# First layer's loop: where the gate product and the projection stand, and how far ahead the decay scans run

## The chip, the core and the metric

The kernel runs on one core of one Trainium2 chip. The metric is the device time of one execution in microseconds (us). TensorE (PE, with PEld for its weight loads), VectorE (DVE), ScalarE (ACT), GpSimd (POOL) and the DMA queue of SyncE (SP) work through their own instructions in order and wait for each other by semaphores.

## What is computed

Two transformer layers on x of 4 batches x 256 tokens x 256 features, each with modulated layer norms. The first layer's attention is a gated delta rule with 32 value heads over 16 key heads; this is where the loop stands:

```
qkvz = h @ W_qkvz                      # q, k, v, z per key head
q, k, v = silu(causal conv of 4 taps over q, k, v)
step:  S = S * alpha_t                 # per token and head; S is 128 x 128
       v_new = (v_t - S'k_t) * beta_t
       S = S + k_t v_new' ;  o_t = S'q_t
og = o * silu(z);  og = og * rsqrt(mean(og*og) + eps) * norm_weight
out = og @ W_out
```

The rest (a feed-forward part with integer weights, a second layer with softmax attention and a sum of eight factors) isn't touched.

## The kernel before

Tokens are cut into two chunks of 128 (c = 0, 1). The recurrence of a chunk is a triangular system, whose inverse is built once per key head for all batches and heads. The loop `for kh in range(16)` has four steps b = 0..3, one per batch (B = 4), and each engine has its own step function: `pe_step`, `act_step`, `dve_step`, `pool_step`. A pass over the four steps is called a round here. The order inside a step is written out by hand; engines meet only at semaphores. Step b = 0 is the one that `merges`: it alone puts the inverse together from 32x32 blocks (`pe_merge_*`, lines 390 to 411), which POOL has computed during the round before (`pool_inverse`, lines 1045 and 1048, tiles Tn and tmp) and which came back by DMA.

In one step a batch is solved (`pe_solve` 0, 1, 2 at line 442; after 0 and 2 ACT copies Y by `act_y`, line 686, after 1 DVE makes R2, line 919), its output is formed (`pe_o` 0 and 1, lines 455 and 457; `dve_og`, line 927, multiplies with the silu of the gate z; `act_ss`, line 714, squares and sums it; `pool_ro`, line 1021, takes the root), and the batch of the step before, `last`, is normalised (`act_ogn`, 722), turned (`pe_ot`, 466; copied by `act_ots`, 745) and projected (`pe_f` 0 and 1, 476), then added up (`dve_acc`, 934). Beside it run preparations of later steps: the product for q and k eight to nine steps ahead (`pe_qk`, 314; `act_tap0` and `dve_tap` form the convolution, then `act_silu_qk`, 660 and 662), the gram matrices (`pe_gram0` at 324, `pe_gram1` at 328 and 332; scaled into BP by `dve_bp`, 915), v three steps ahead (`pe_v`, 344; turned by `pe_vt`, 366; copied by `act_vs`, 678) and the gate product z (`pe_z`, 354; `act_silu_z`, 667, into the tile named hT). The v and z products share a PSUM bank: `pe_z` waits for the taps of v, and the next `pe_v` for the silu of z.

`dve_bp` needs the decays E1 and E2 of its batch, running products of alpha that `dve_scan` makes by `tensor_tensor_scan` (lines 866 and 869): two of 128x256 and two of 128x128 for a batch, called a set here. There is one pair of buffers, so that the scans of a batch wait for the BP of the batch before it.

At the end of step 0 ACT and DVE also split the weights of later heads in a high and a low part (lines 732, 727 on ACT; 878, 874 on DVE). In steps 2 and 3 ACT copies half of the inverse turned (`act_turn`, 739). The loop of the ACT step that follows a merging step begins with `act_ss(*last)`, in front of `act_y` 0:

```
if last and merges(last[2]):
    act_ss(*last)
```

## Time and profile before

| | us |
|---|---|
| median of 3 runs (1215.8 to 1224.04) | 1216.73 |
| the profiled execution, its own time | 1216.18 |
| its span, first to last instruction | 1214.5 |
| one round of the loop, 577.20 to 633.37 | 56.17 |

The span begins at the first instruction; 1.7 us of the execution lie around it. Rounds are told apart by the first gram matmul of step 0. A row of a time line gives the start in us from the span's start, the time, engine, line, operation, output <- inputs and how many were put together; in square brackets how long the engine sat idle before it and for whom. A matmul's own time is longer than the distance to the next one's start, since they overlap: what a group takes of PE is the distance between starts.

### The profile page before, as it was taken

The page shows a single profiled execution, that of the slowest core. Times are in us where ns is not written, and L with a number is a line of the kernel's source. Part 1 is how long each engine was busy: PE and PEld are TensorE (multiplying, and loading weights), DVE is VectorE, ACT ScalarE, POOL GpSimd, SP SyncE. Part 2 cuts the span into 40 slices and gives each one's busy share as a digit, 9 for nine tenths or more (in the row PEclk, how much of TensorE's full clock was granted, in tenths as well). Part 3 has the DMA queues.
Part 4 walks back from the last instruction along what each step waited for, and adds up shares of the span by engine and source line. Part 5 has one row for each costly group of instructions (what it writes and reads, how often), then busy time and mean ns, then how long its engine had stood idle before and what let it go on. Part 6 is the DMA issues. An engine that isn't in the chain of part 4 may idle for free. (4 is left out here: it accounts for less than half of the span.)

```text
span 1214.5 us, 30101 instructions
## 1 busy us (share of the span) xinstructions
PE 1125.3 (93%) x10744; PEld 980.4 (81%) x10744; DVE 903.9 (74%) x2304; ACT 824.7 (68%) x2225; POOL 724.4 (60%) x1187
## 2 busy tenths in 40 slices
PE   7795799999999999999999999999998798998975
PEld 6685688888888888988888888888887787776654
DVE  6878587988888897989897898888792525328764
ACT  6333577777777777777777777877775665219983
POOL 3274677787878776877778787777676702114211
PEclk9778899999999999999999999999998989999998
DMA  5211315522231313141322313131215130002000
GB/s 185 64 57 29 94 39 82 56 69 58 65 92 41 82 41 82 41 106 45 82 55 67 62 62 92 40 82 32 48 34 158 27 112 1 1 6 70 2 19 18
DMA packets 140868, 72.80 MB, mean 60 GB/s; under 512 B 114184, under 2 KB 130064, under 8 KB 138800
## 3 DMA queue, kind: packets, MB, share of 16 engines
q1 hardware_dynamic: 140720, 70.88, 23.4%
q8 instruction: 86, 1.41, 0.5%
q14 instruction: 62, 0.51, 0.2%
HBM read 57.06 MB, written 13.78 MB: 58 GB/s over the span
## 5 line engine op out<-in xcount | busy, mean ns | idle before, releaser
L1048 POOL TENSOR_TENSOR Tn<-Tn,tmp 64x31 f32<-64x31 f32 (+15 forms) x496 | 275.8, 556 | 38.9
L1045 POOL TENSOR_TENSOR tmp<-DT,Tn 64x31 f32<-64x31 f32 (+15 forms) x496 | 244.7, 493 | 51.0 <-DMA DT<-blk_in_scratch 17.0
L855 DVE SCALAR_TENSOR_TENSOR cv<-bank,cw,cv 128x255 f32<-128x255 f32 (+2 forms) x384 | 155.0, 472 | 74.0 <-ACT cv L653 73.9
L855 DVE SCALAR_TENSOR_TENSOR cqk<-bank,cw,cqk 128x255 f32<-128x255 f32 (+2 forms) x384 | 155.2, 473 | 26.2 <-ACT cqk L653 26.2
L1021 POOL TENSOR_TENSOR ro<-ss,mhalf 128x4 f32<-128x4 f32 x64 | 71.9, 1124 | 139.2 <-issue 90.6
L915 DVE SCALAR_TENSOR_TENSOR BP<-bank,cj,E 128x512 f32<-128x512 f32 (+1 forms) x256 | 140.4, 611 | 2.4 <-DVE cj L900 0.2
L476 PE MATMUL bank<-wo,OTs 128*128 128x256 f32 x512 | 125.2, 388 | 0.0
L476 PEld LDWEIGHTS bank<-wo,OTs 128*128 128x128 f32 x512 | 94.1, 194 | 11.6 <-issue 0.5
L455 PE MATMUL bank<-Y,BP 128*128 128x128 f32 x512 | 95.7, 290 | 2.3 <-issue 0.5
L686 ACT ACTIVATE Y<-bank 128x256 f32<-128x256 f32 x128 | 48.9, 382 | 72.0 <-PE bank L442 70.4
L722 ACT ACTIVATE ogn<-og,ro 128x128 f32<-128x128 f32 x256 | 81.7, 395 | 22.7 <-POOL ro L1021 22.6
L314 PE MATMUL bank<-hh,wqk_hi 128*128 128x256 f32 x256 | 81.0, 316 | 12.6 <-DVE wqk_lo L874 9.3
L714 ACT ACTIVATE junk<-og 128x129 f32<-128x129 f32 x256 | 79.5, 310 | 17.0 <-issue 4.8
L344 PE MATMUL bank<-hh,wvz_hi 128*128 128x256 f32 x256 | 80.5, 314 | 4.8 <-ACT hT L667 4.8
L455 PEld LDWEIGHTS bank<-Y,BP 128*128 128x128 f32 x512 | 73.0, 193 | 14.3 <-ACT Y L686 13.7
L354 PE MATMUL bank<-wvz_hi,hh 128*128 128x256 f32 x256 | 82.6, 323 | 1.5
L927 DVE SCALAR_TENSOR_TENSOR og<-bank,vsc,hT 128x256 f32<-128x256 f32 x128 | 55.5, 475 | 32.6 <-PE bank L457 32.6
L314 PE MATMUL bank<-hh,wqk_lo 128*128 128x256 f32 x256 | 75.2, 294 | 0.0
L314 PE MATMUL bank<-hl,wqk_hi 128*128 128x256 f32 x256 | 75.0, 293 | 0.0
L324 PE MATMUL bank<-sqk 128*128 128x512 f32 x128 | 67.9, 612 | 6.3 <-DVE BP L915 4.9
L344 PE MATMUL bank<-hl,wvz_hi 128*128 128x256 f32 x256 | 73.4, 287 | 0.0
L344 PE MATMUL bank<-hh,wvz_lo 128*128 128x256 f32 x256 | 73.4, 287 | 0.0
(209 smaller groups left out, 3292.9 us busy)
## 6 DMA issues: line engine op xcount, KB each, us to landing
rvz<-in_L_attn_W_qkvz SPq DMA_DIRECT2D x16, 512.0 KB, 3.6
x<-alpha_scratch SPq DMA_DIRECT2D x8, 1024.0 KB, 5.0
alb<-alpha_scratch SPq DMA_DIRECT2D x7, 1024.0 KB, 5.9
rqk<-in_L_attn_W_qkvz SPq DMA_DIRECT2D x16, 256.0 KB, 2.6
wo<-in_L_attn_W_out SPq DMA_DIRECT2D x16, 256.0 KB, 3.8
blk_in_scratch<-BP SPq DMA_DIRECT2D x256, 16.0 KB, 1.5
DT<-blk_in_scratch SPq DMA_DIRECT2D x16, 256.0 KB, 3.4
tinv_scratch<-Tn SPq DMA_DIRECT2D x32, 128.0 KB, 2.1
```

The lines of the kernel that those rows point to most:

```text
L314: last = nc.tensor.matmul(bQK[:, t * T:(t + 1) * T], wqk[p][w][:, k, t * DK:(t + 1) * DK], h[:, k, b * T:(b + 1) * T], start=(k + n == 0), ...
L344: last = nc.tensor.matmul(bV[:, t * T:(t + 1) * T], wvz[p][w][:, k, t * DK:(t + 1) * DK], h[:, k, b * T:(b + 1) * T], start=(k + n == 0), ...
L354: last = nc.tensor.matmul(bZ[:, c * 256:(c + 1) * 256], h[:, k, b * T + c * P:b * T + (c + 1) * P], wvz[p][w][:, k, R * DK:2 * R * DK], st ...
L455: last = nc.tensor.matmul(o, block_of(kh, b, h, 0, 0, c), Y[:, 0, h, :], start=True, stop=(c == 0))
L476: last = nc.tensor.matmul(bF[:, c * D:(c + 1) * D], OTs[:, h, c, :], wo[p][:, h, :], start=(h == 0), stop=(h == R - 1))
L714: nc.scalar.activation(junk[:], og[b % 2][:, c, h, :], ACT.Square, accum_out=ss[b % 2][:, n:n + 1]).then_inc(sem("ss"), 1)
L722: nc.scalar.activation(ogn[:, c, h, :], og[b % 2][:, c, h, 0:DK], ACT.Copy, scale=ro[b % 2][:, n:n + 1]).then_inc(sem("ogn"), 1)
L855: nc.vector.scalar_tensor_tensor(d, bk[:, t * T:(t + 1) * T - s], cw[p][:, first + t, TAPS - 1 - s:TAPS - s], d, ALU.mult, ALU.add).then_i ...
L915: nc.vector.scalar_tensor_tensor(dst, g, cj[i][:, c, h:h + 1], e, ALU.mult, ALU.mult).then_inc(sem("bp"), 1)
L1021: nc.gpsimd.tensor_tensor(ro[b % 2][:], ss[b % 2][:], mhalf[:, 0:4], ALU.pow).then_inc(sem("ro"), 1)
L1045: pool_step_done(nc.gpsimd.tensor_tensor(t, Dm[:, j, j + 1:BLK].unsqueeze(2).broadcast_to([SLOTS, r, c]), Tn[:, j, 0:c].unsqueeze(1).broad ...
L1048: pool_step_done(nc.gpsimd.tensor_tensor(Tn[:, j + 1:BLK, 0:c], Tn[:, j + 1:BLK, 0:c], t, ALU.subtract), kh * NTS + 2 * j + 4)
```

## The change

- `pe_z` and `act_silu_z` of a batch leave the end of their step. They run in the next step (`late_z`): behind solve 0 in steps 2 and 3, in front of the q/k product in step 0 of the next round. Step 1 has none, since step 0 still does its own z inside the merge. The turn `pe_vt` and the q/k product thus stand 12 matmuls later in their step.
- The projection is put in two parts: `pe_f` 0 between `pe_o` 0 and `pe_o` 1, `pe_f` 1 behind. For that `act_ots` moves ahead of `act_y` 1, and the first tap of v (`act_tap0`) behind both.
- `pe_o` 1 of step 0 moves into step 1, between `pe_gram0` and `pe_gram1`.
- The wait for `square_qk` moves from `pe_gram0` into `pe_gram1`; sqq and og have one buffer in place of two.
- E1 and E2 get two pairs of buffers. The scans of a round stand thus: all four of batch 0 at the top of step 0, all four of batch 1 before R2 of step 0, all four of batch 2 behind it; E1 of batch 3 before R2 of step 1, E2 of batch 3 behind R2 of step 2. Before, they were: batch 0 at the top of step 0, E1 of batch 1 before and E2 of batch 1 behind R2 of step 0, batch 2 and batch 3 at the top of steps 2 and 3.
- In step 0 the splits on DVE stand in front of `dve_og`, not behind.

The hunks left out rename buffers and take the last z product of batch 2 out of the lead-in before the loop (step 0 of round 0 does it).

```diff
@@ -221,7 +221,7 @@
             nw = sb("nw", [P, 1], ctx=s1)
             ones = sb("ones", [P, 1], ctx=s1)
             npow = sb("npow", [P, 4], ctx=s1)
-            sqq = [sb(f"sqq{i}", [P, 2, T], ctx=s1) for i in range(2)]
+            sqq = sb("sqq", [P, 2, T], ctx=s1)
             cv = sb("cv", [P, R, T], ctx=s1)
             sv = [sb(f"sv{i}", [P, R, T], ctx=s1) for i in range(2)]
             nrm = [sb(f"nrm{p}", [P, B, 4], ctx=s1) for p in range(2)]
@@ -230,8 +230,8 @@
             rcn = [sb(f"rcn{i}", [P, 2], ctx=s1) for i in range(2)]
             cj = [sb(f"cj{i}", [P, NC, R], ctx=s1) for i in range(2)]
             vsc = [sb(f"vsc{p}", [P, B, 4], ctx=s1) for p in range(2)]
-            E1 = sb("E1", [P, R, T], ctx=s1)
-            E2 = sb("E2", [P, R, P], ctx=s1)
+            E1 = [sb(f"E1_{i}", [P, R, T], ctx=s1) for i in range(2)]
+            E2 = [sb(f"E2_{i}", [P, R, P], ctx=s1) for i in range(2)]
 
             BP1 = sb("BP1", [P, RING - B, 6 * R, P], ctx=s1)
 
...
@@ -319,7 +319,6 @@
             def pe_gram0(kh, p, b):
                 i = b % 2
                 wait(nc.tensor, "silu_qk", at(kh, b, 1, 1))
-                wait(nc.tensor, "square_qk", at(kh, b, 1, 1))
                 wait(nc.tensor, "bp", at(kh, b, 4))
                 nc.tensor.matmul(bG1[:], sqk[i][:, 0, 0:P], sqk[i][:].rearrange("p x t -> p (x t)"), start=True, stop=True)
 
@@ -327,9 +326,10 @@
                 i = b % 2
                 nc.tensor.matmul(bG2[:, 0:2 * P].rearrange("p (x t) -> p x t", x=2), sqk[i][:, 0, P:T], sqk[i][:, :, P:T],
                                  start=True, stop=True)
+                wait(nc.tensor, "square_qk", at(kh, b, 1, 1))
                 for q in range(2):
                     for c in range(NC):
-                        last = nc.tensor.matmul(bG2[:, 256 + 2 * q + c:257 + 2 * q + c], sqq[i][:, 1 - q, c * P:(c + 1) * P],
+                        last = nc.tensor.matmul(bG2[:, 256 + 2 * q + c:257 + 2 * q + c], sqq[:, 1 - q, c * P:(c + 1) * P],
                                                 ones[:, 0:1], start=True, stop=True)
                 last.then_inc(sem("gram"), 1)
 
@@ -584,21 +584,27 @@
             def merges(b):
                 return b == 0
 
+            def late_z(kh, p, b):
+
+                return beside(kh, p, b, LEAD_VZ - 1) if not merges((b - 1) % B) else None
+
             def pe_step(kh, p, b):
                 qk, gram, vz, vt, last = (beside(kh, p, b, n) for n in (LEAD_QK, LEAD_GRAM, LEAD_VZ, LEAD_VZ - 1, -1))
+                zl = late_z(kh, p, b)
                 now = at(kh, b, 1)
                 if gram:
                     pe_gram0(*gram)
+                if last and merges(last[2]):
+                    pe_o(*last, 1)
+                if gram:
                     pe_gram1(*gram)
-                if not merges(b):
-                    pe_solve(kh, p, b, 0)
-                    pe_behind_solve(kh, b)
-                    if vt:
-                        pe_vt(*vt, now - 1)
-                if qk:
-                    pe_qk(*qk, 0)
-                    pe_qk(*qk, 1)
                 if merges(b):
+                    if zl:
+                        pe_z(*zl, 0)
+                        pe_z(*zl, 1)
+                    if qk:
+                        pe_qk(*qk, 0)
+                        pe_qk(*qk, 1)
                     if vz:
                         pe_v(*vz, 0)
                     pe_merge_diag(kh)
@@ -626,8 +632,17 @@
                         pe_vt(*vt, now)
                     pe_solve(kh, p, b, 2)
                     pe_o(kh, p, b, 0)
-                    pe_o(kh, p, b, 1)
                 else:
+                    pe_solve(kh, p, b, 0)
+                    pe_behind_solve(kh, b)
+                    if zl:
+                        pe_z(*zl, 0)
+                        pe_z(*zl, 1)
+                    if vt:
+                        pe_vt(*vt, now - 1)
+                    if qk:
+                        pe_qk(*qk, 0)
+                        pe_qk(*qk, 1)
                     pe_solve(kh, p, b, 1)
                     if vz:
                         pe_v(*vz, 0)
@@ -636,14 +651,11 @@
                     pe_ot(*last, 2 * (now + 3))
                     pe_solve(kh, p, b, 2)
                     pe_o(kh, p, b, 0)
+                    pe_f(*last, 0)
                     pe_o(kh, p, b, 1)
                     if kh == NKH - 1 and b == B - 1:
                         pe_turn_w1(12, 3)
-                    pe_f(*last, 0)
                     pe_f(*last, 1)
-                    if vz:
-                        pe_z(*vz, 0)
-                        pe_z(*vz, 1)
 
 
             def act_tap0(kh, p, b, name, bk, dst, first):
@@ -659,7 +671,8 @@
                 wait(nc.scalar, "square_qk", at(kh, b, 1))
                 nc.scalar.activation(sqk[b % 2][:], cqk[:], ACT.Silu).then_inc(sem("silu_qk"), 1)
                 wait(nc.scalar, "silu_qk", at(kh, b, 1, 1))
-                nc.scalar.activation(sqq[b % 2][:], sqk[b % 2][:], ACT.Square).then_inc(sem("square_qk"), 1)
+                wait(nc.scalar, "gram", at(kh, b, 1))
+                nc.scalar.activation(sqq[:], sqk[b % 2][:], ACT.Square).then_inc(sem("square_qk"), 1)
 
             def act_silu_z(kh, p, b):
                 wait(nc.scalar, "z_mm", at(kh, b, 1, 1))
...
@@ -817,30 +833,25 @@
                     splits(kh, p, b, act_split_qk, act_split_vz)
                 else:
                     act_y(kh, p, b, 0)
+                    if zl:
+                        act_silu_z(*zl)
                     if vt:
                         act_vs(*vt)
-                    if not merges(last[2]):
-                        act_ogn(*last)
+                    act_ogn(*last)
                     if qk:
                         act_tap0(*qk, "qk", bQK, cqk, 0)
-                    if merges(last[2]):
-                        act_ogn(*last)
                     act_before_ots(kh, b)
+                    act_ots(*last)
+                    act_y(kh, p, b, 1)
                     if vz:
                         act_tap0(*vz, "v", bV, cv, 2)
-                    act_y(kh, p, b, 1)
-                    act_ots(*last)
                     if kh + 1 < NKH and b >= 2:
                         act_turn(kh + 1, b - 2)
                     if qk:
                         act_silu_qk(*qk)
                     if vz:
                         act_silu_v(*vz)
-                    if vz and kh >= NKH - 2:
-                        act_silu_z(*vz)
                     act_ss(kh, p, b)
-                    if vz and kh < NKH - 2:
-                        act_silu_z(*vz)
                     if kh == NKH - 1 and b == B - 1:
                         act_turned_w1(12, 3)
 
@@ -860,13 +871,13 @@
                     wait(nc.vector, "alb_act", b + 1)
                 elif b == 0 and n == 0:
                     wait(nc.vector, f"alb_in{p}", (kh - p) * 8 + 16 * p)
-                h = n % R
-                wait(nc.vector, "bp", at(kh, b, 4))
+                h, i = n % R, b % 2
+                wait(nc.vector, "bp", at(kh, b, 4, -4))
                 if n < R:
-                    nc.vector.tensor_tensor_scan(E1[:, h, :], alb[p][:, h, b * T:(b + 1) * T], eye[:], 0.0,
+                    nc.vector.tensor_tensor_scan(E1[i][:, h, :], alb[p][:, h, b * T:(b + 1) * T], eye[:], 0.0,
                                                  ALU.mult, ALU.add).then_inc(sem("scan"), 1)
                 else:
-                    nc.vector.tensor_tensor_scan(E2[:, h, :], alb[p][:, h, b * T + P:(b + 1) * T], ident, 0.0,
+                    nc.vector.tensor_tensor_scan(E2[i][:, h, :], alb[p][:, h, b * T + P:(b + 1) * T], ident, 0.0,
                                                  ALU.mult, ALU.add).then_inc(sem("scan"), 1)
 
             def dve_split_qk(kh, p):
...
@@ -923,8 +934,8 @@
                     wait(nc.vector, "o", at(kh, b, 2, 2))
                     wait(nc.vector, "silu_z", at(kh, b, 1, 1))
                     if c == 0:
-                        wait(nc.vector, "ogn", at(kh, b, 4, -4))
-                    nc.vector.scalar_tensor_tensor(og[b % 2][:, c, :, 0:DK], bO[:, c * 256:(c + 1) * 256].rearrange("p (h d) -> p h d", h=R),
+                        wait(nc.vector, "ogn", at(kh, b, 4))
+                    nc.vector.scalar_tensor_tensor(og[:, c, :, 0:DK], bO[:, c * 256:(c + 1) * 256].rearrange("p (h d) -> p h d", h=R),
                                                    vsc[p][:, b, c:c + 1], zs[:, b, c, :].rearrange("p (h d) -> p h d", h=R), ALU.mult, ALU.mult).then_inc(sem("og"), 1)
 
             def dve_acc(kh, p, b):
@@ -948,17 +959,26 @@
                     for n in range(lo, hi):
                         dve_scan(*g, n)
 
+                ahead = [beside(kh, p, b, LEAD_GRAM + n) for n in range(3)]
+
+                def scans_ahead(n, lo=0, hi=2 * R):
+                    if ahead[n]:
+                        scans(ahead[n], lo, hi)
+
                 if gram and gram[2] == 0:
                     dve_bet(gram[0], gram[1])
                 if gram:
-                    if not merges((b - 1) % B):
-                        scans(gram, 0, 2 * R)
+                    if merges(b):
+                        scans_ahead(0)
                     dve_scales(*gram)
-                    dve_bp(*gram, 0)
-                if gram:
-                    dve_bp(*gram, 1)
+                    for c in range(NC):
+                        dve_bp(*gram, c)
                 if not merges(b):
+                    if b == 1:
+                        scans_ahead(2, 0, R)
                     dve_r2(kh, p, b)
+                    if b == 2:
+                        scans_ahead(1, R, 2 * R)
                 for taps in (taps_v, taps_qk) if merges(b) else (taps_qk, taps_v):
                     for n in range(1, TAPS):
                         taps(n)
@@ -967,14 +987,11 @@
                 if last:
                     dve_acc(*last)
                 if merges(b):
-                    ahead = beside(kh, p, b, LEAD_GRAM + 1)
-                    if ahead:
-                        scans(ahead, 0, R)
+                    scans_ahead(1)
                     dve_r2(kh, p, b)
-                    if ahead:
-                        scans(ahead, R, 2 * R)
+                    scans_ahead(2)
+                    splits(kh, p, b, dve_split_qk, dve_split_vz)
                     dve_og(kh, p, b)
-                    splits(kh, p, b, dve_split_qk, dve_split_vz)
 
 
             def dve_dequant(i, m):
...
```

## Rows read from the trace of the kernel before

**Rows 1.** The page: busy time, and granted clock of PE in 40 slices.
```profile
PE 1125.3 (93%) x10744; PEld 980.4 (81%) x10744; DVE 903.9 (74%) x2304; ACT 824.7 (68%) x2225; POOL 724.4 (60%) x1187
...
PEclk9778899999999999999999999999998989999998
```

**Rows 2.** Busy time by stretch: step 2, and the whole round.
```profile
608.60:620.99 12.39, 12.30 (x91) 11.02 (x90) 11.45 (x28) 9.76 (x27) 9.73 (x16) 1.00 0.12 27
...
577.20:633.37 56.17, 55.65 (x578) 49.70 (x577) 48.42 (x113) 43.12 (x113) 42.29 (x70) 1.00 0.26 66
```

**Rows 3.** Time line of PE: end of step 0, step 1, step 2.
```profile
593.94 0.71 PE L442 MATMUL bank<-R,UT 128*128 128x128 f32 x4
...
596.12 1.02 PE L324 MATMUL bank<-sqk 128*128 128x512 f32 x2
...
600.61 0.61 PE L442 MATMUL bank<-Y,BP 128*128 128x128 f32 x4
...
605.44 1.89 PE L476 MATMUL bank<-wo,OTs 128*128 128x256 f32 x8
...
608.60 0.59 PE L324 MATMUL bank<-sqk 128*128 128x512 f32 x1
...
615.42 0.61 PE L442 MATMUL bank<-R,UT 128*128 128x128 f32 x4
615.86 1.12 PE L455 MATMUL bank<-Y,BP 128*128 128x128 f32 x6
...
617.50 1.89 PE L476 MATMUL bank<-wo,OTs 128*128 128x256 f32 x8
```

**Rows 4.** Time line of PE's weight loads: the turn in step 1.
```profile
602.87 0.20 PEld L466 LDWEIGHTS bank<-eye,ogn 128*128 128x128 f32 x2 [0.42 <-ACT ogn L722]
```

**Rows 5.** Time line of DVE: end of step 0, start of step 1.
```profile
590.86 1.62 DVE L866 TENSOR_TENSOR_SCAN E<-alb,eye 128x256 f32<-128x256 f32 x2
593.46 0.42 DVE L919 TENSOR_TENSOR R<-Vs,bank 128x256 f32<-128x256 f32 x1 [0.98 <-PE bank L442]
593.80 1.59 DVE L869 TENSOR_TENSOR_SCAN E<-alb,eye 128x128 f32<-128x128 f32 x2
...
597.11 1.22 DVE L878 TENSOR_TENSOR wvz_lo<-rvz,wvz_hi 128x1024 fp32r<-128x1024 f32 x1
598.24 0.68 DVE L874 TENSOR_TENSOR wqk_lo<-rqk,wqk_hi 128x512 fp32r<-128x512 f32 x1
```

**Rows 6.** Time line of DVE: the scans at the top of step 3.
```profile
620.69 1.26 DVE L866 TENSOR_TENSOR_SCAN E<-alb,eye 128x256 f32<-128x256 f32 x2
621.87 0.71 DVE L869 TENSOR_TENSOR_SCAN E<-alb,eye 128x128 f32<-128x128 f32 x2
```

**Rows 7.** Time line of DVE and POOL in step 0 of an earlier round.
```profile
422.38 2.11 DVE L866 TENSOR_TENSOR_SCAN E<-x,eye 128x256 f32<-128x256 f32 x2
422.97 0.97 POOL L1048 TENSOR_TENSOR Tn<-Tn,tmp 64x240 f32<-64x240 f32 x1
```

**Rows 8.** Time line of POOL: its last work on blocks in step 0.
```profile
595.19 0.68 POOL L1048 TENSOR_TENSOR Tn<-Tn,tmp 64x252 f32<-64x252 f32 x1
```

**Rows 9.** Time line of ACT: around the start of step 1, and in step 2.
```profile
595.68 1.07 ACT L732 ACTIVATE wvz_hi<-rvz 128x1024 fp32r<-128x1024 f32 x1
...
597.14 0.32 ACT L714 ACTIVATE junk<-og 128x129 f32<-128x129 f32 x1
...
598.95 0.38 ACT L686 ACTIVATE Y<-bank 128x256 f32<-128x256 f32 x1
...
616.34 0.68 ACT L745 ACTIVATE OTs<-bank,nw 128x512 f32<-128x512 f32 x1
617.05 1.12 ACT L739 ACTIVATE DT<-Tn 64x512 f32<-64x512 f32 x1
```

**Rows 10.** Time line of PE: the first merge matmul of round 14.
```profile
916.61 0.18 PE L390 MATMUL bank<-U,BP 32*32 32x32 f32 x1 [1.57 <-issue]
```

**Rows 11.** Busy time by stretch, ten us behind that; clock in column PEclk.
```profile
917.30:927.30 10.00, 10.00 (x159) 8.46 (x154) 3.12 (x7) 4.25 (x9) 8.55 (x19) 0.50 0.12 21
```

More of the change, by code:

```diff
@@ L254, in build @@
             Y = sb("Y", [P, NC, R, DK], ctx=s1)
-            og = [sb(f"og{i}", [P, NC, R, DK + 1], ctx=s1) for i in range(2)]
+            og = sb("og", [P, NC, R, DK + 1], ctx=s1)
             ogn = sb("ogn", [P, NC, R, DK], ctx=s1)
@@ L713, in act_ss @@
                         wait(nc.scalar, "ss", at(kh, b, 4, n))
-                        nc.scalar.activation(junk[:], og[b % 2][:, c, h, :], ACT.Square, accum_out=ss[b % 2][:, n:n + 1]).then_inc(sem("ss"), 1)
+                        nc.scalar.activation(junk[:], og[:, c, h, :], ACT.Square, accum_out=ss[b % 2][:, n:n + 1]).then_inc(sem("ss"), 1)
             def act_ogn(kh, p, b):
@@ L721, in act_ogn @@
                         n = c * R + h
-                        nc.scalar.activation(ogn[:, c, h, :], og[b % 2][:, c, h, 0:DK], ACT.Copy, scale=ro[b % 2][:, n:n + 1]).then_inc(sem("ogn"), 1)
+                        nc.scalar.activation(ogn[:, c, h, :], og[:, c, h, 0:DK], ACT.Copy, scale=ro[b % 2][:, n:n + 1]).then_inc(sem("ogn"), 1)
             def act_split_qk(kh, p):
@@ L1338, in _ @@
                             pe_vt(0, 0, b - 1, 0)
-                for c in range(NC):
-                    pe_z(0, 0, LEAD_VZ - 1, c)
                 pe.wait_ge(sem("modT"), 2 * MODS)
```

10 lines of the change are left out of this document (6 added, 4 removed).

## Prediction, made before the changed kernel ran

> **What bounds the kernel now.** I read the page first: PE is busy 93% of the span, DVE 74%, ACT 68%, POOL 60%, and PE's clock stays at its upper level of 2.4 GHz through the middle of the span [rows 1]. The loop is most of the time, and its rounds are nearly all alike: 56.17 us, of which PE's records cover 55.65 [rows 2]. So PE bounds the loop, and what can be won is only what lies between its groups of matmuls. As a matmul's record is longer than its issue distance, short waits hide under "busy"; I look for them in the distances between starts.
>
> Three such waits are in the rows. First, `pe_o` 1 waits for the copy Y. Solve 2 has four matmuls in 615.86 - 615.42 = 0.44 us, so 0.11 each; the twelve of `pe_o` 0 and 1 should take 1.33 and take 617.50 - 615.86 = 1.64 [rows 3]. The wait costs 0.31, and it stands in all four steps. Second, in steps 2 and 3 the z product waits for the taps of v: projection and z take 620.99 - 617.50 = 3.49 there, but 608.60 - 605.44 = 3.16 in step 1 [rows 2, 3]: 0.33 each. Third, the turn in step 1 waits 0.42 for the normalised output [rows 4]. Together 4 x 0.31 + 2 x 0.33 + 0.42 = 2.32 us of a round. That is the prize, 4% of the round.
>
> **The change part by part.** PE's own work stays: every matmul is moved, none added. The z product (3.16 less the projection's eight matmuls, recorded as 1.89 with a drain of 0.17, so 1.44 us) leaves step 1 and enters step 0, nothing else changes hands but `pe_o` 1 of step 0 (eight matmuls, 0.9 us).
>
> *Gains.* `pe_f` 0 is four matmuls, 0.87 us, in front of `pe_o` 1: Y copy (0.38 us, [rows 9]) is covered, 0.31 gone in steps 1 to 3; in step 0 `pe_gram0` covers it (two matmuls, recorded 1.02 with the drain of 0.17, so 0.85, [rows 3]), 0.31 gone. z behind solve 0 finds its taps done in the step before, 0.33 gone twice. The 0.42 of step 1 goes into what comes below. All 2.32 are taken off.
>
> *New small waits.* `pe_f` 0 needs OTs. In step 2's terms the turn ends at 615.42, its last matmul drains about 0.17 later (0.61 against 0.44, [rows 3]), OTs takes 0.68 [rows 9] and is ready at 616.3; solve 2 and `pe_o` 0 end at 616.31 and the weights want to be loaded 0.1 earlier. Wait 0.15 (0 to 0.2), three times: 0.45. With the q/k product 1.5 us later and the first tap of v and the turned copy (1.12, [rows 9]) in front of it on ACT, the silu of q/k ends about when the next `pe_gram0` wants it in steps 2 and 3: 0.05 each (0 to 0.3), 0.1. The other queues: SP issues nothing new; the turned copy of step 3 is some 1.8 us later, and the blocks that come back from it by DMA with it, but the merge that reads them is 1.5 us later too.
>
> *The scans.* This is where I expect the gain to be spent. A set costs 1.9 us on DVE when POOL is quiet (1.26 and 0.71, [rows 6]). In step 0, with POOL at its blocks, the pair of E1 took 1.62 and the pair of E2 1.59 [rows 5], in another round E1 2.11, while the POOL instruction beside it took 0.97 where its like takes some 0.68 [rows 7, 8]. So these scans and POOL's block instructions exclude each other in turns. The change moves the scans of batch 2 and half of batch 1 from quiet places into that stretch. I take 3.2 for a set there, bounds 1.9 and 3.7.
>
> The Trainium skill (page "SBUF — State Buffer", section "Who interferes with whom") says that a DVE instruction with two SBUF inputs contends with a GpSimd instruction that reads SBUF, and that whoever starts first holds the pair for the whole instruction. The rows on the scans agree. By the same rule the two weight splits, tensor_tensor with both inputs in SBUF, would wait for POOL as well; no row shows that, since POOL was idle then (its last block instruction ended at 595.87, [rows 8]). This speaks against the change; what it would give is the third rival below.
>
> Set T at solve 2 of step 0 (593.94, [rows 3]) and follow step 0 into step 1.
> - *R2.* The E1 scans start at T - 3.08 [rows 5]. Now a whole set is there: over at T + 0.1, R2 (0.42, begun 0.07 before that) at T + 0.5, where it was T - 0.06. New wait on PE 0.56 (0 if the set takes 1.9, as then it ends before solve 1; 1.06 at 3.7). PE is waiting in solve 2 and all behind it moves along, so T' from here on is the new start of solve 2.
> - *og.* Behind R2 come another set (T' - 0.14 to T' + 3.05), the splits (1.13 + 0.67 = 1.8 from the starts and the last time in [rows 5]), with half a turn of POOL 0.3, and then og of chunk 0, 0.47: T' + 5.6; before, the first square of it could start at T + 3.2 (597.14, [rows 9]). POOL is still at its blocks then: it ended at T + 1.9 [rows 8], begins the round later, and loses more to eight scans.
> - *Y of step 1.* ACT has `act_ss` in front of `act_y` 0 in step 1; from the first square to Y it is 1.81, and Y takes 0.38 [rows 9]. So Y is ready at T' + 7.8. What is queued behind it on ACT is silu, Vs and the normalised output, and PE waits for Y at solve 1.
> - *When PE wants it.* `pe_gram0` starts at T' + 0.98 (2.18 from 593.94 to 596.12, less `pe_o` 1 with its wait, 1.20), solve 1 is 4.49 behind it [rows 3], and `pe_o` 1 adds 0.9: T' + 6.4, weights 0.1 earlier. New wait 1.6. Lower bound: scans undisturbed, the splits start when the high part is ready (596.75 = T + 2.81, [rows 9]), Y at T' + 7.3, wait 1.05. Upper: a set of 3.7 and a full POOL instruction in front of each split, Y at T' + 9.2, wait 3.0.
> - *Behind it.* The turn's wait of 0.42 is absorbed: normalising ends about when PE, late itself, arrives. DVE catches up in steps 1 to 3, which have lost scans.
>
> **Sum.** A round: -2.32 + 0.45 + 0.10 + 0.56 + 1.6 = +0.4 us, bounds -2.32 + 1.05 + 0.3 = -1.0 and -2.32 + 4.06 + 1.2 = +2.9. Thirteen rounds (1 to 13) have it in full: +5 us (-13 to +38). In round 0 the added z goes under a wait for blocks, about -1.5. Rounds 14 and 15 have no scans; PE waits there for blocks anyway (1.57, [rows 10]), which hides z before and after: -1 (-4 to +1). Against the profiled execution's 1216.2, half a microsecond under the median: 1216.2 + 5 - 2.5 = 1219, rounded up to 1220 since the upper bounds are wider.
>
> **Rivals.**
> - *Clean gain.* Scans and splits don't hold up R2 and og, or ACT's late start is made up before solve 1. For it: DVE has 7.7 us free in a round [rows 2], and most of its work is early. Against it: the chain T' to Y is in order on two engines, and even undisturbed it is 1.05 late. If it holds, 2.32 less 0.4 for OTs and silu: -1.9 x 13 - 2.5 = -27, 1189.
> - *Nothing.* The waits only change places, sum within 0.1 a round: 1214 to 1217. It lies in my forecast's range and is counted there.
> - *Slower: the lock of POOL and DVE in step 0.* Sets of 3.7 and splits behind POOL as well. R2 1.06 late, Y 3.0 late: +2.3 a round, 13 rounds +30, less 2.5: 1244. It decides against the change from the point where the two new waits of step 0/1 pass 1.8 us together. For it: [rows 5, 7]; against: POOL has few instructions left by the splits. The Trainium skill's rule above points here.
> - *Slower: the clock.* A wait of 1.57 at a merge [rows 10] was followed by a clock of 0.50, that is 1.2 GHz, for ten us [rows 11]. My wait of 1.6 in step 1 is as long, in denser work. If it brings even 3 us at half clock each round: +3 x 13, about 1260.
>
> **How the numbers follow.** Forecast with its bounds 0.52, clean gain 0.17, lock 0.23, clock 0.08. The three runs spread over 0.7%; 1% (12.2 us) is about what a measurement here can tell from no change. Of the forecast's 0.52 some 0.43 are within 1% (1204.6 to 1228.9), 0.04 below, 0.05 above; clean gain is below; lock mostly above (0.20), clock above. Faster 0.21, same 0.46, slower 0.33. The range of 8 in 10 is 1193 to 1250; the likeliest case by itself 1208 to 1232.
>
> **What would show it.** In the changed profile: no idle time of PE's loads at line 455 for Y; instead idle time at line 442 for Y of about 1.6 in step 1 and a wait for R2 in step 0 that is longer by about 0.6; scans of step 0 at 0.8 to 1.1 us each instead of 0.35 to 0.65 (half of a pair in [rows 6]); rounds of 56.6 us with steps 2 and 3 at 12.0. I am wrong if scans in step 0 run undisturbed, if og comes before T' + 4.3, or if the half clock shows up inside the loop.

## The result, and the profile after

The changed kernel takes 1224.69 us (median of 17 runs, 1219.35 to 1230.36), the kernel before 1218.59 (17 runs, 1212.37 to 1224.92). The ratio is 1.0049, 95% interval 1.0033 to 1.0065: half a per cent slower, within 1% of no change, and 5 us above the forecast of 1220.

The profiled execution took 1228.10 us (span 1226.4), the second slowest of the 17. In its page the busy share of PE fell by a point against [rows 1], because the span grew:

```profile
PE 1125.4 (92%) x10744; PEld 987.0 (80%) x10744; DVE 923.3 (75%) x2304; ACT 820.2 (67%) x2225; POOL 724.7 (59%) x1186
...
PEclk8866899999999999999999999999998999999996
```

The same round as in [rows 2], cut at the starts of the four first gram products (busy time by stretch; the last row is the round):

```profile
579.76:599.45 19.69, 19.20 (x317) 17.07 (x317) 16.93 (x37) 14.12 (x35) 16.80 (x29) 1.00 0.42 109
599.45:612.15 12.70, 11.84 (x86) 10.65 (x86) 12.20 (x26) 9.61 (x28) 7.92 (x9) 1.00 0.26 69
612.15:624.14 11.99, 11.99 (x90) 10.95 (x88) 10.70 (x27) 9.41 (x26) 10.20 (x17) 1.00 0.04 6
624.14:636.22 12.08, 12.08 (x89) 11.01 (x88) 9.78 (x26) 9.69 (x27) 7.01 (x17) 1.00 0.24 52
579.76:636.22 56.46, 55.10 (x577) 49.68 (x576) 49.61 (x112) 42.84 (x113) 41.94 (x69) 1.00 0.27 66
```

Before, the steps took 18.92, 12.48, 12.39 and 12.38 us, 56.17 together; now 19.69, 12.70, 11.99 and 12.08, 56.46. Steps 2 and 3 are 0.4 and 0.3 shorter; PE's records now cover them wholly. Step 1 gave its gate product (1.5 us) to step 0 and took `pe_o` 1 (0.9) from it; without new waits it would be near 11.4, as the first experiment shows, and it is 12.70.

The time line of PE shows both new waits, where [rows 3] had neither:

```profile
597.42 0.60 PE L366 MATMUL bank<-eye,sv 128*128 128x128 f32 x4
598.51 0.71 PE L442 MATMUL bank<-R,UT 128*128 128x128 f32 x4 [0.49 <-DVE R L930]
...
604.78 0.28 PE L314 MATMUL bank<-hl,wqk_hi 128*128 128x256 f32 x1
605.87 0.71 PE L442 MATMUL bank<-Y,BP 128*128 128x128 f32 x4 [0.81 <-ACT Y L699]
...
608.05 0.66 PE L466 MATMUL bank<-eye,ogn 128*128 128x128 f32 x4
...
609.49 1.13 PE L476 MATMUL bank<-wo,OTs 128*128 128x256 f32 x4
```

Idle time in brackets starts at the end of a record, which is some 0.17 behind the point where the next product could have been issued, so the wait is read from distances between starts. The four turned copies (line 366) in front of solve 2 of step 0 start 0.11 apart, the last at 597.75. From there to solve 2 at 598.51 it is 0.77 us, where the kernel before had 0.35: the wait for R2 costs 0.42 more. From the last q/k product to solve 1 of step 1 it is 605.87 - 604.78 = 1.09, and 0.12 where PE does not wait: the wait for Y costs 0.97.

What made them late stands in DVE's time line ([rows 5] before):

```profile
595.02 1.67 DVE L877 TENSOR_TENSOR_SCAN E<-alb,eye 128x256 f32<-128x256 f32 x2
596.61 1.53 DVE L880 TENSOR_TENSOR_SCAN E<-alb,eye 128x128 f32<-128x128 f32 x2
598.07 0.39 DVE L930 TENSOR_TENSOR R<-Vs,bank 128x256 f32<-128x256 f32 x1
598.38 1.75 DVE L877 TENSOR_TENSOR_SCAN E<-alb,eye 128x256 f32<-128x256 f32 x2
600.05 1.52 DVE L880 TENSOR_TENSOR_SCAN E<-alb,eye 128x128 f32<-128x128 f32 x2
601.50 1.19 DVE L889 TENSOR_TENSOR wvz_lo<-rvz,wvz_hi 128x1024 fp32r<-128x1024 f32 x1
602.62 0.68 DVE L885 TENSOR_TENSOR wqk_lo<-rqk,wqk_hi 128x512 fp32r<-128x512 f32 x1
603.22 0.86 DVE L938 SCALAR_TENSOR_TENSOR og<-bank,vsc,hT 128x256 f32<-128x256 f32 x2
```

These are two sets of scans of 3.1 us each with R2 between them, then both splits, then og. ACT's squares of og stand ahead of Y in its queue, so Y follows og (ACT; [rows 9] before):

```profile
603.77 0.31 ACT L727 ACTIVATE junk<-og 128x129 f32<-128x129 f32 x1 [1.93 <-issue]
...
605.45 0.36 ACT L699 ACTIVATE Y<-bank 128x256 f32<-128x256 f32 x1
```

POOL's last instruction on blocks in this step ([rows 8] before):

```profile
600.61 0.68 POOL L1065 TENSOR_TENSOR Tn<-Tn,tmp 64x252 f32<-64x252 f32 x1
```

**Where the 11.9 us between the two profiled spans lie**, from the starts of the first merge products of the rounds (L390) and of the first down product of the MLP behind the loop, before and after:

- Up to the merge of round 2, 244.2 and 246.3: +2.1. The loop starts 1.8 later, round 0 is 6.0 shorter, round 1 is 4.7 longer, and the merge of round 2 has 1.5 more in front of it, the moved gate product. Of the 4.7, step 2 of round 1 has 3.8. That step differs between executions of either order: 13.71 us in last_round (experiment 9, the same code there) against 16.45 here, and 16.04 in quiet_before (experiment 5), which has the old order. last_round starts its loop 2.0 us later instead and begins round 2 only 0.5 earlier.
- Rounds 2 to 12, to 862.7 and 869.0: +4.2.
- Rounds 13 and 14, to 971.7 and 978.0: nothing. Round 14 is a balance, though: the wait for Y in step 1 grows by 1.6 (shown under experiment 1), the distances in front of solve 1 in steps 2 and 3 shrink from 2.00 to 0.73 each, and the clock was granted at half for 10.2 us of that round before and for 6.8 after.
- Round 15 up to the down product, to 1032.6 and 1042.0: **+3.1**, with 6.8 us at half clock in both.
- From there to the end: +2.5, at a mean granted clock of 0.95 against 0.98, in code that the change doesn't touch.

The medians differ by 6.1 us. The rounds (0.3 us in each of thirteen, so 4) and the 3 of round 15 come to 7, without the first and the last item.

Round 15 is the part that the prediction did not have. PE's time line there:

```profile
1002.49 1.13 PE L476 MATMUL bank<-wo,OTs 128*128 128x256 f32 x4 [0.37 <-ACT OTs L758]
...
1009.84 1.12 PE L466 MATMUL bank<-eye,ogn 128*128 128x128 f32 x4 [1.48 <-ACT ogn L735]
...
1017.42 0.71 PE L442 MATMUL bank<-Y,BP 128*128 128x128 f32 x4 [1.39 <-ACT Y L699]
...
1021.82 1.13 PE L476 MATMUL bank<-wo,OTs 128*128 128x256 f32 x4 [0.47 <-ACT OTs L758]
```

and ACT's, where the weight copies of the MLP stand ahead of OTs:

```profile
1009.70 1.70 ACT L769 ACTIVATE area_a<-bank 128x256 f32<-128x256 f32 x6
1011.28 0.69 ACT L758 ACTIVATE OTs<-bank,nw 128x512 f32<-128x512 f32 x1
```

In this round there are no products of later steps to fill PE, so it waits for a chain of work: turn, OTs, `pe_f` 0, `pe_o` 1, og, squares, `ro`, ogn, and the next turn. `pe_f` 0 and its OTs were not in that chain before.

### The profile page after: what moved, and what is told of

Its sections match the earlier page's. It is cut to its first block and busy times, and to the rows that moved or that the text cites. A ratio compares the mean times of both kernels' runs of the same rounds, so it can differ in the third digit from the quotient of the medians.

```text
span 1226.4 us, 30158 instructions
## 1 busy us (share of the span) xinstructions
PE 1125.4 (92%) x10744; PEld 987.0 (80%) x10744; DVE 923.3 (75%) x2304; ACT 820.2 (67%) x2225; POOL 724.7 (59%) x1186
## 5 line engine op out<-in xcount | busy, mean ns | idle before, releaser
L1062 POOL TENSOR_TENSOR tmp<-DT,Tn 64x31 f32<-64x31 f32 (+15 forms) x496 | 250.3, 505 | 49.2 <-DMA DT<-blk_in_scratch 15.0
L1038 POOL TENSOR_TENSOR ro<-ss,mhalf 128x4 f32<-128x4 f32 x64 | 67.6, 1057 | 151.8 <-issue 95.8
L476 PE MATMUL bank<-wo,OTs 128*128 128x256 f32 x512 | 138.2, 398 | 3.6 <-ACT OTs L758 3.6
L476 PEld LDWEIGHTS bank<-wo,OTs 128*128 128x128 f32 x512 | 90.4, 194 | 16.1 <-ACT OTs L758 4.2
L455 PE MATMUL bank<-Y,BP 128*128 128x128 f32 x512 | 89.5, 277 | 0.1
L455 PEld LDWEIGHTS bank<-Y,BP 128*128 128x128 f32 x512 | 78.3, 194 | 9.7 <-ACT Y L699 3.8
L323 PE MATMUL bank<-sqk 128*128 128x512 f32 x128 | 71.1, 638 | 10.0 <-DVE BP L926 10.0
L354 PE MATMUL bank<-wvz_hi,hl 128*128 128x256 f32 x256 | 73.8, 288 | 0.0
L354 PE MATMUL bank<-wvz_lo,hh 128*128 128x256 f32 x256 | 73.7, 288 | 0.0
```

The source lines that it names most:

```text
L323: nc.tensor.matmul(bG1[:], sqk[i][:, 0, 0:P], sqk[i][:].rearrange("p x t -> p (x t)"), start=True, stop=True)
L354: last = nc.tensor.matmul(bZ[:, c * 256:(c + 1) * 256], h[:, k, b * T + c * P:b * T + (c + 1) * P], wvz[p][w][:, k, R * DK:2 * R * DK], st ...
L455: last = nc.tensor.matmul(o, block_of(kh, b, h, 0, 0, c), Y[:, 0, h, :], start=True, stop=(c == 0))
L476: last = nc.tensor.matmul(bF[:, c * D:(c + 1) * D], OTs[:, h, c, :], wo[p][:, h, :], start=(h == 0), stop=(h == R - 1))
L1062: pool_step_done(nc.gpsimd.tensor_tensor(t, Dm[:, j, j + 1:BLK].unsqueeze(2).broadcast_to([SLOTS, r, c]), Tn[:, j, 0:c].unsqueeze(1).broad ...
```

## The experiments

All ratios are to the kernel before, which ran beside each of them: its median is 1219.46 us (21 runs) for experiments 1, 2, 6 and 8, and 1219.05 us (17 runs) for 3, 7, 9 and 10. The timed variants have 4 to 12 runs each.

**1. scans_back: the scans and splits where they were.** The changed kernel, with

```
 step 0, top:     - scans_ahead(0)  if b == 0      + scans(gram, all) if the step before isn't 0
 steps 1, 2:      - scans_ahead(2, 0, R) / scans_ahead(1, R, 2R) around dve_r2
 step 0, end:     - scans_ahead(1); dve_r2; scans_ahead(2); splits; dve_og
                  + scans_ahead(1, 0, R); dve_r2; scans_ahead(1, R, 2R); dve_og; splits
```

> The changed kernel with the scans and the two DVE weight splits where they stood before (batch 0 at the top of step 0, batch 1 around R2 of step 0, batches 2 and 3 at the top of steps 2 and 3; splits behind og); the two pairs of buffers stay. Theory (the scans ahead cost what the other two parts win): R2 of step 0 is ready as early as before, so the 0.42 us that PE waits longer there goes, and og comes some 1.7 us earlier, so the 1.1 us wait for Y at solve 1 of step 1 goes; steps 2 and 3 stay at 12.0, since the taps of v are wanted only in the step behind. A round is 56.5 - 1.5 = 55.0, 13 rounds -20 us against the changed kernel, -14 against before: ratio to before 0.988. Rival (the rounds' length comes from the projection and the z product, the scans are hidden): ratio stays at 1.005, and steps 2 and 3 grow by 0.3 to 0.5 each as DVE is late again.

Measured: 1198.36 us, ratio 0.9831 (0.9804 to 0.9858), better than the 0.988 expected. The steps (busy time by stretch):

```profile
564.03:583.31 19.28, 19.20 (x317) 17.14 (x317) 15.29 (x35) 14.17 (x34) 16.45 (x29) 1.00 0.42 108
583.31:594.68 11.37, 11.37 (x86) 10.59 (x85) 9.79 (x23) 9.91 (x28) 8.12 (x10) 1.00 0.28 77
...
564.03:618.75 54.72, 54.64 (x578) 49.65 (x577) 47.93 (x112) 42.97 (x113) 41.88 (x69) 1.00 0.27 68
```

The round is 1.74 us shorter than after and 1.45 shorter than before. Step 0 lost 0.41 and step 1 lost 1.33: the two new waits and what follows on them. Steps 2 and 3 stay as they were. 13 rounds x 1.74 = 22.6, and the medians differ by 26.3; rounds 14 and 15 are shorter too, by 4.9 and 2.2 us in the profiled executions, but those of scans_back ran at full clock and those of the changed kernel did not (0.94 in round 14, 0.95 in round 15), so this is not all due to the edit. So the reordering of PE, with that of ACT which goes with it, is worth 1.7%, and the placing of DVE's work takes it all back and half a per cent more.

In round 14 the same order of og and splits is seen alone, as it has no scans. DVE in the changed kernel:

```profile
941.11 1.23 DVE L889 TENSOR_TENSOR wvz_lo<-rvz,wvz_hi 128x1024 fp32r<-128x1024 f32 x1 [2.90 <-ACT wvz_hi L745]
942.25 0.87 DVE L938 SCALAR_TENSOR_TENSOR og<-bank,vsc,hT 128x256 f32<-128x256 f32 x2
```

The split waits for ACT's high part with og behind it in the queue. PE, in the changed kernel and then in the kernel before:

```profile
944.90 1.22 PE L442 MATMUL bank<-Y,BP 128*128 128x128 f32 x4 [3.41 <-ACT Y L699]
```

```profile
938.49 0.71 PE L442 MATMUL bank<-Y,BP 128*128 128x128 f32 x4 [1.81 <-ACT Y L686]
```

From the last turned copy to solve 1 it is 3.68 us in the changed kernel and 2.09 where og is ahead of the splits, in the kernel before as in scans_back. In the changed kernel the clock was at half for 3.4 us from this solve on (the four products record 1.22 in place of 0.71). The same wait was not followed by half clock in quiet_after and proj_whole.

**2. og_first: og ahead of the splits, the scans as changed.**

```
 step 0, end:     - splits(...); dve_og(...)
                  + dve_og(...); splits(...)
```

> The changed kernel with one line moved: in step 0, DVE does og ahead of the two weight splits, behind the scans of batch 2. Theory: og of chunk 0 starts 1.7 us earlier (T' + 3.0 in place of 4.7), ACT's squares and Y with it, and the 1.1 us wait at solve 1 of step 1 goes; the 0.42 longer wait for R2 stays; DVE's work up to the next BP is the same, so nothing else is later. Round 55.4 to 55.6, 13 rounds -12 us against the changed kernel: ratio to before 0.995. Rival (that wait would be taken over by the turn of the output or by R2 of step 1): less than 0.4 a round, ratio above 1.001.

Measured: 1217.6 us, ratio 0.9984 (0.9968 to 1.0); round of 56.34 us. The expected gain of 0.9 to 1.1 us a round did not come: it is 0.12, as the rival had it. PE, step 1:

```profile
604.94 0.61 PE L442 MATMUL bank<-Y,BP 128*128 128x128 f32 x4
...
608.50 0.71 PE L442 MATMUL bank<-R,UT 128*128 128x128 f32 x4 [1.07 <-DVE R L930]
```

The wait for Y is gone, and one for R2 of step 1 has come, 1.34 us from the turn's last product to solve 2 where it was 0.11. DVE runs without a gap from R2 of step 0 (598.07 in the changed kernel, 598.12 here) to R2 of step 1 (608.00 and 608.05): 9.93 us of work in either order. Y's wait had only hidden that. The medians of this kernel and the changed one lie 7 us apart: the rounds explain 1.6 of it, and the shorter wait of round 14 (2.09 for 3.68) another 1.6; the rest was not located. The profiled execution can't show it, as it is the slowest of this kernel's twelve (1225.98), with 17.1 us at half clock in round 14.

**3. og_r2_first: in addition, the two long scans of step 1 behind R2.**

```
 step 1:          - scans_ahead(2, 0, R); dve_r2
                  + dve_r2; scans_ahead(2, 0, R)
```

> The kernel after, with og ahead of the splits in step 0 (as og_first) and, in step 1, the two long scans behind R2 in place of ahead of it. og_first took the wait for Y in step 1 away (1092 ns from the last qk product to the first solve product became 118) and a wait for R2 of step 1 came in its place (109 became 1344 ns). Theory: VectorE's queue from R2 of step 0 to R2 of step 1 (9.93 us in both) is longer than the 8.7 us that TensorE needs between the two, so any order of what lies between gives the same; 1.27 us of scans taken out of this stretch should take all of the 1.23 us away: round of 55.1 us (54.9 to 55.4) where og_first had 56.33 and after 56.46, a ratio of 0.986 (0.984 to 0.990). Rival: the wait only moves on, to the transposes of ogn or to the tap products of step 1 behind the scans, and the round stays at 55.9 or more, ratio above 0.993.

Measured: 1206.57 us, ratio 0.9897 (0.9864 to 0.993).

```profile
569.99:589.67 19.68, 19.19 (x317) 17.13 (x317) 16.58 (x37) 14.16 (x34) 16.82 (x29) 1.00 0.41 108
589.67:601.49 11.82, 11.55 (x87) 10.41 (x85) 11.71 (x26) 9.31 (x28) 8.70 (x10) 1.00 0.27 75
...
569.99:625.65 55.66, 54.91 (x577) 49.57 (x576) 48.78 (x112) 42.86 (x113) 42.31 (x70) 1.00 0.26 67
```

```profile
601.49 1.12 PE L323 MATMUL bank<-sqk 128*128 128x512 f32 x2 [0.27 <-ACT sqk L672]
```

0.7 of the 1.2 us came back, not all. DVE's queue between the two R2s was the bound, but the scans now delay the taps of q and k, and the gram of the next step waits for its silu: it starts 0.65 behind the last projection product, and 0.22 where nothing waits. What is left against scans_back is 0.4 in step 0 (R2), 0.45 in step 1 and 0.1 in step 2. The time is in the expected range, the round 0.3 above it.

**4. quiet_after and 5. quiet_before: POOL out of the way.** In each, the block instructions of POOL work on one element; the inverse of the 64-wide blocks is left out, so these two compute something else, and only the waits of a round are read. The cut below is in both (left out: the operands that are made one element wide with it).

```
-                    r, c = BLK - 1 - j, j + 1
+                    r, c = 1, 1
```

> The kernel after, with GpSimd's block instructions of the first layer (the inverse of the 64-wide blocks) cut to one element each; it leaves out the inverse, so its output is not the reference's, and its time is only read for the waits of a round. Theory: the two sets of scans of step 0 take 3.2 and 3.2 us in after because they and GpSimd's block instructions, which run beside them, slow each other down (GpSimd's take 0.86 to 0.98 there and 0.6 to 0.7 elsewhere); alone they take what they take in other steps, 1.26 for the two long and 0.71 for the two short ones, 1.97 us a set. Then R2 of step 0 starts early enough (distance of 768 ns to the solve product falls to 350 or less) and the wait for Y in step 1 (1092 ns) falls to 118 to 300: a round of 54.7 to 55.3 us. Rival: the scans are slow there for another reason (the first after a long idle stretch, VectorE's own order), the sets stay at 3 us and more, and the round at 56 to 56.5.

> The control for quiet_after: the kernel before with the same cut of GpSimd's block instructions (the inverse left out). Theory: its scans of step 0 (1.62 and 1.59 us for two each beside GpSimd) fall to 1.26 and 0.71, but nothing waits for them, so the round of 56.17 us changes by less than 0.3. Rival: without GpSimd's chain the round falls by as much as in quiet_after, 1 us or more, and quiet_after then says nothing of the scans.

Measured, one profiled execution each: 1207.37 and 1207.81 us. Rounds of the changed and of the old kernel with POOL quiet:

```profile
573.92:629.83 55.91, 55.09 (x577) 49.70 (x577) 46.04 (x112) 42.88 (x113) 20.42 (x70) 1.00 0.28 67
```

```profile
575.57:631.74 56.17, 55.64 (x578) 49.69 (x577) 46.17 (x113) 43.12 (x113) 20.64 (x69) 1.00 0.26 66
```

The control stays at 56.17 to the hundredth, as expected, so what changes in the other comes of the new placement of DVE's work beside POOL. DVE and PE of quiet_after:

```profile
589.12 1.26 DVE L877 TENSOR_TENSOR_SCAN E<-alb,eye 128x256 f32<-128x256 f32 x2
590.31 0.71 DVE L880 TENSOR_TENSOR_SCAN E<-alb,eye 128x128 f32<-128x128 f32 x2
...
595.04 1.23 DVE L889 TENSOR_TENSOR wvz_lo<-rvz,wvz_hi 128x1024 fp32r<-128x1024 f32 x1 [1.08 <-ACT wvz_hi L745]
```

```profile
599.44 0.71 PE L442 MATMUL bank<-Y,BP 128*128 128x128 f32 x4 [0.70 <-ACT Y L699]
```

A set takes 1.9 us in place of 3.1: the scans and POOL's block instructions do slow each other. The distance in front of solve 2 goes back to 0.35, so the new wait for R2 is gone. But Y's wait falls from 0.97 to 0.86 only (0.98 from the last q/k product, less 0.12), against what was expected: the first split then waits 1.08 for ACT's high part. It starts 2.84 behind solve 2 of step 0 (595.04 - 592.20), and in the changed kernel 2.99 behind it (601.50 - 598.51). So contention costs this kernel 0.55 us a round, not the 1.2 to 1.8 expected of it; most of Y's wait is due to og standing behind two splits whose input ACT delivers late.

The Trainium skill (page "SBUF — State Buffer", section "Who interferes with whom") has the rule that a VectorE instruction with two SBUF inputs and a reading GpSimd instruction hold each other off. For the scans the two runs agree, 3.1 against 1.9 us a set. For the splits the changed kernel tests nothing: POOL had ended at 601.29, before they began, and they take 1.19 and 0.68 there, 1.22 and 0.68 before [rows 5].

**6. scans_alone: only DVE's new placement, on the kernel before.** The same edits to `dve_step` as in the change, with the pairs E1 and E2, but PE's and ACT's order of before. og and the squares have single buffers, with the wait of ACT's square for the gram that this needs; in the profiled round no instruction is held up by either.

> The kernel before with only the scans changed: two pairs of E buffers, one of og and sqq, the scans and splits of DVE where the change puts them; z and the projection as before. Theory: R2 of step 0 0.4 late; Y of step 1 is ready at T' + 7.3, here wanted at T' + 6.6 as all of the output product is still in step 0, wait 0.7; the 0.42 of the turn in step 1 is absorbed by it; DVE of steps 2 and 3 is 1.9 us earlier, so the 0.33 wait for the taps of v goes twice. Sum +0.4 + 0.7 - 0.4 - 0.66 = about 0 a round, ratio 0.999 to 1.004. Rival (scans ahead are the useful part, as they free DVE where it is full): -0.7 a round or better, ratio 0.992.

Measured: 1254.24 us, ratio 1.0298 (1.0274 to 1.0323), far outside both the expectation and its rival. The round:

```profile
597.93:657.10 59.17, 56.18 (x579) 49.67 (x578) 48.79 (x112) 43.11 (x113) 41.36 (x69) 1.00 0.25 63
```

```profile
615.52 0.71 PE L442 MATMUL bank<-R,UT 128*128 128x128 f32 x4 [0.93 <-DVE R L920]
...
622.77 0.71 PE L442 MATMUL bank<-Y,BP 128*128 128x128 f32 x4 [0.41 <-ACT Y L687]
...
643.18 0.38 PE L354 MATMUL bank<-wvz_hi,hh 128*128 128x256 f32 x1 [0.83 <-DVE cv L856]
```

The placement costs 3.0 us a round here and 1.74 in the changed kernel. The waits for R2 (1.20 from the turned copy, 0.35 before; the added 0.85 is twice that of the changed kernel) and Y (0.69, 0.12 before) are there again, and the turn waits 0.27 longer. The rest, 0.52 in step 1 and 0.77 in step 2, is the z product behind the projection: it waits for v's taps (0.55 and 1.21 from the last projection product; 0.03 and 0.44 before), and DVE reaches them later. That is a price which the moved z spares the changed kernel; the expectation had forgotten it.

**7. z_back: scans_back with the gate product back at the end of the step.**

```
 pe_step:         - if zl: pe_z(*zl, 0); pe_z(*zl, 1)   (before the q/k product)
                  + if vz: pe_z(*vz, 0); pe_z(*vz, 1)   (behind pe_f 1)
 act_step:        silu of z back to the end of the step
```

> The kernel with scans and splits placed as before (scans_back, 0.9831, round of 54.72 us), with the gate product and its silu back at the end of the step, as before; the split projection, OTs ahead of Y, the output behind the next gram, and both pairs of buffers stay. Theory: the move of the gate product is what pays in this change: behind the projection it waits for VectorE's v taps (0.41 us in steps 2 and 3 before), and what TensorE now saves ahead of it on Y's wait it waits there in addition. Round of 55.5 to 56.1 us, ratio 0.990 to 0.997. Rival: the gain of scans_back comes from the projection and the gram's order, and the gate product can stand at either place: round of 54.7 to 55.0, ratio 0.983 to 0.986.

Measured: 1237.07 us, ratio 1.0173 (1.0125 to 1.0221).

```profile
583.70:601.43 17.73, 17.66 (x306) 15.59 (x305) 13.31 (x29) 12.10 (x28) 14.74 (x29) 1.00 0.33 86
...
583.70:640.80 57.10, 55.08 (x578) 49.54 (x577) 48.05 (x112) 43.01 (x113) 41.42 (x69) 1.00 0.26 65
```

```profile
613.75 0.39 PE L354 MATMUL bank<-wvz_hi,hh 128*128 128x256 f32 x1 [0.79 <-DVE cv L863]
```

The round is 2.38 us longer than in scans_back, twice what was expected, and 0.9 longer than before. From the last projection product to z it is 1.17 us in step 1 and 0.96 in steps 2 and 3, 0.03 when nothing is waited for. Two things may add up: what PE saves ahead of z it waits there, and OTs ahead of Y puts v's first tap on ACT later. Both are read from the order of the queues, and neither was tried alone. So the parts of the change on PE and ACT have no worth of their own: without the moved z the other moves are a loss, and with it they pay. The moved z without the others was not run.

**8. proj_whole: the changed kernel with both halves of the projection behind both outputs.**

```
-                    pe_f(*last, 0)
                     pe_o(kh, p, b, 1)
+                    pe_f(*last, 0)
                     pe_f(*last, 1)
```

> The changed kernel with the projection in one piece again in steps 1 to 3: output product 0 and 1, then both halves of the projection (on ACT OTs stays ahead of Y). Theory: the wait for Y between the two halves of the output product comes back, longer than before since OTs (0.68) is now ahead of it on ACT: 0.4 to 0.6 in each of three steps, less the 0.15 for OTs: +0.9 to +1.3 a round, 13 rounds +12 to +17 us; ratio to before 1.015 to 1.019. In round 15, where OTs is late behind the weight copies, og no longer hangs on it: -1 to -2 us there. Rival (the split hides nothing, Y was covered anyway): ratio 1.003 to 1.006.

Measured: 1225.89 us, ratio 1.0056 (1.0036 to 1.0075), in the range of the rival; the expected +0.9 to +1.3 a round is +0.46.

```profile
582.69:639.61 56.92, 55.12 (x577) 49.86 (x576) 49.03 (x113) 42.81 (x113) 42.06 (x70) 1.00 0.26 66
```

```profile
612.52 0.49 PE L455 MATMUL bank<-Y,BP 128*128 128x128 f32 x2 [0.15 <-ACT Y L699]
```

But the split does not simply do nothing. The round is 0.46 longer without it (Y's wait is back), 6 us in 13 rounds; rounds 13 to 15 up to the first down product take 166.0 us where the changed kernel takes 173.0. Of these 7 us round 14 has 3.8, and there the changed kernel had 6.8 us at half clock and proj_whole none, so most of them can be the clock. Round 15 has 3.2, with 6.8 and 3.4 us at half clock. So the split gains 6 us inside and loses some at the end; how much, the next two runs tell.

**9. last_round and 10. scans_back_tail: round 15 as before.** In the changed kernel, and in scans_back:

```
 if kh == NKH - 1:   pe_o 1; pe_f 0; pe_f 1     (else pe_f 0; pe_o 1; pe_f 1)
 if kh == NKH - 1:   act_y 1 ahead of act_ots   (else behind it)
```

> The kernel after, with one difference in round 15 alone: both halves of the projection stand behind both outputs again, and ScalarE evicts Y ahead of OTs; rounds 0 to 14 are those of after. Theory: in round 15 the chain ot, OTs, first half of the projection, second output, og, squares, ro, ogn, ot is closed by the split, and OTs comes late there because ScalarE evicts weight copies ahead of it. The stretch from the first merge product of round 15 (978.0 in after) to the first down product of the MLP (1042.0) took 64.0 us in after and 60.9 before, so it should take 60.9 again: 3.1 us less, a ratio to before of about 1.0025 (1.000 to 1.004) where after had 1.0049. Rival: these 3.1 us come from something else in the stretch (a clock dip, the late start), and the ratio stays at 1.004 to 1.006 with the stretch at 63.5 to 64.5.

> The kernel with the scans and splits placed as before (0.9831 of before) and the same difference in round 15 as in last_round. Theory: its stretch from the first merge product of round 15 to the first down product, 61.8 us, loses the same waits (OTs 0.8 and 0.6, ogn 0.6, solve 0.86), some 2.5 to 3 us, so the ratio is 0.981 (0.979 to 0.983). Rival: with og ahead of the splits the chain is short enough and nothing is gained, 0.983 or more.

Measured: last_round 1219.76 us, ratio 1.0011 (0.9987 to 1.0034); scans_back_tail 1193.22 us, ratio **0.9798** (0.9768 to 0.9829), the fastest of all. Round 15 from the first merge product to the first down product, in scans_back and in scans_back_tail, both at full clock:

```profile
946.30:1008.10 61.80, 52.22 (x519) 44.60 (x519) 25.18 (x62) 35.80 (x105) 9.51 (x16) 1.00 0.18 55
```

```profile
949.60:1007.50 57.90, 52.43 (x518) 44.54 (x518) 25.16 (x62) 36.08 (x105) 8.74 (x16) 1.00 0.18 59
```

It is 3.9 us less, with no difference in the clock. In the changed kernel it went from 64.0 to 59.6, 4.4 less, at mean clocks of 0.95 and 0.97; in proj_whole, where only PE's order differs, the stretch takes 60.8. The chain is confirmed, and it is dearer than expected (3.1 in the changed kernel, 2.5 to 3 in scans_back). The interval of scans_back_tail overlaps that of scans_back, so that it is faster by the ratio is likely and not shown; that the stretch is shorter is shown.

## Why the prediction was right

The forecast (1220, with +0.4 us a round) held, through its own mechanism: what PE wins is spent on the waits for R2 and for Y that DVE's new order makes. That +0.4 and the measured +0.29 lie so close is in part luck, as the errors of several terms cancel.

- *The prize and the gains.* 2.32 us of waits less 0.55 for OTs and silu should leave 1.77. scans_back, which has only these, measures 1.45. Steps 2 and 3 were forecast at 12.0 each and take 11.99 and 12.08. The silu of q/k was put at 0.05 a time and costs 0.17: 0.07 in the distance to the gram, and 0.10 in the gram's own second product. OTs costs what was forecast (0.15, of which 0.10 comes behind the wait).
- *R2.* Forecast 0.56, measured 0.42. The set was put at 3.2 and takes 3.1.
- *Y of step 1.* Forecast 1.6 with a lower bound of 1.05; measured 0.97 and 0.10 in the product behind it. That is at its lower bound. PE wanted Y at T' + 6.4 as forecast (604.90). og's first half was put at T' + 5.6, and its first square came at T' + 5.3: **the term that was mis-sized is the half turn of POOL (0.3) in front of the splits**, which did not occur, and there was 0.15 too much on ACT. The reasoning of the lower bound was that og is late even with undisturbed scans, since the splits start when the high part is ready (T' + 2.81). quiet_after showed just that: T' + 2.84.
- *The turn in step 1.* Its 0.42 was said to be absorbed; half of it, 0.21, is still there (0.33 from the last v product to the turn, 0.12 undisturbed).
- *The sum of a round.* Forecast +0.4, measured +0.29. The new waits, with what is left of the turn's, were forecast 0.46 too dear, the gains 0.3 too good.
- *The tail*, forecast -1, measured +3.1: **this step failed.** Rounds 14 and 15 were said to wait for blocks anyway, which hides z. It was not asked what each part of the change does where there is no next work. Splitting the projection puts OTs, late on ACT behind weight copies, into the chain that carries the last round: mending it takes 3.9 us off at full clock (scans_back_tail), 4.4 in the changed kernel. And in round 14 og behind the splits makes PE wait 3.68 for Y where it was 2.09.
- *The distance to the median.* Of the terms between the forecast of 1220 and the median of 1224.69 the tail is the largest, 4.1 us. The base adds 2.4: the forecast starts from the profiled 1216.2, and the kernel before has a median of 1218.59 over 17 runs. The rounds, 1.3 us cheaper than forecast, and the rounding up to 1220 take some of it back.
- *Round 0*, forecast -1.5: it is 6.0 shorter, with the loop's start 1.8 later and round 1 4.7 longer, so that round 2 begins 0.5 later than before. How much of this is the change and how much the execution is open.
- *The rivals.* A clean gain of 27 us was named for the case that DVE's work doesn't hold up R2 and og; scans_back realises it, with 21 us, and 26 after the last round is mended. The lock needed splits behind POOL, and POOL was done. The clock stays at 1.00 from round 2 to round 13; the wait in step 1 brought no half clock there.
- *The signs.* In the round shown the loads at line 455 sit idle for Y for 0.2 us in one place, where it was 0.9 us in four places. The scans of step 0 take 0.76 to 0.88 us each (0.8 to 1.1 expected), the round 56.46 (56.6). Solve 1 waits for Y as named, but 0.97 in place of 1.6.

## What to carry to other kernels

A reordering on the engine that bounds the kernel and one on an engine that serves it, made in the same change, should be priced and run apart: here they are worth -1.7% and +2.2%, and the second alone, on the old order, +3.0%. In a queue that feeds the bounding engine, put what it waits for (og) ahead of what nobody waits for soon (splits), above all when the latter itself waits for a third engine. And price each part of a loop's edit again in its first and last round, where the work that hides a wait is missing.

## What the runs showed of the hardware that was not expected

A wait of PE costs more than its distance shows: the product behind the one that waited is issued 0.21 us later and not 0.11 (128x128 products). Four such products record 0.71 behind a wait and 0.61 without one (608.50 and 604.94 in og_first). It is 0.10 us a wait, as much as the shortest waits themselves.

Two engines that slow each other need not cost what the slowing adds: the two sets of scans grew by 1.2 us each, and the round by 0.55, because the splits behind them in DVE's queue start almost as early either way (2.84 and 2.99 behind solve 2): with fast scans the first of them waits for ACT.

Executions of the changed kernel spread from 1219.35 us at a mean granted clock of 0.967 to 1230.36 at 0.959. Round 14 shows where such a spread can come from: og_first and og_r2_first run the same code in it, and it took 56.0 us with 17.1 us of it at half clock in the one and 49.2 us at full clock in the other. An effect of 3 us is therefore read from stretches of traces at the same clock, and not from two times.
